# A two-stage image kernel on one core: the next image's norm, projection and lower levels moved into the last four units of the image before

## The chip, the cores and the metric

One core of a Trainium2 chip. The metric is the device time in microseconds (us) of one execution of the whole program on 16 images. PE is the matmul engine, DVE the vector engine, ACT the scalar engine, POOL the GpSimd engine, SP the engine that issues the DMAs here.

## The reference

x has shape (16, 256, 32, 32), float32. Two residual blocks follow each other:

```python
x = x + conv(gn(x))      # per image: softmax keys give a 7x7 filter for each channel, depthwise convolution
x = x + ssm_block(gn(x)) # gn: group norm, 32 groups
# ssm_block:
xz = in_w @ x; x, z = split(xz)          # 128 channels each
f1 = c1_w @ x                            # 1024 positions
f2 = conv2s2(f1); f3 = conv2s2(f2)       # 256 and 64 positions: the lower levels
# for each level and direction (6 scans), 16 states n:
delta = softplus(dt_w @ (xw @ f) + dtb)
h = h * exp(delta * A_n) + delta * B_n * f ; y += h * C_n
y = layernorm(y + D * f)
out = out_w @ (y1 * silu(z))             # y1 gathers the upsampled lower levels
```

## The kernel before, in words

The five engines run programs written out by hand and meet at counted semaphores. `stages` (L1424) calls a body for each image: 37 units (`NU`), then a bridge. A body works on three images at once: i is in its scans, j = i+1 is in its convolution, m = i+2 is in the preparation of its convolution weights. The bodies are (none, none, 0), (none, 0, 1), fourteen turns of a loop with all three, (14, 15, none) and (15, none, none). So image j's feature maps must be ready when the body's bridge ends, since its units come next.

A unit k is a part of image i's scans. Unit 0 is the third level (64 positions, all 16 states and both directions), units 1 to 4 the second level, units 5 to 36 the first level, one state and one direction each. In a unit:

- SP brings the rows B and C, broadcast to 128 partitions, into rings of 2 (bb) and 3 (cb); `get_b`, `get_c`.
- ACT computes exp(delta A) for unit k+1 in two halves (`decay`, L1173) into the PSUM tile slot_b. Each half waits until DVE's scan of unit k that reads the same bank is over.
- POOL multiplies B with u for unit k+1 (`inputs`, L1315 and L1318) and adds the products of unit k-1 to y (`gather`, L1338 and L1343).
- DVE runs two scans (`scan`, L552) and two products with C (`weigh`, L561).
- PE runs the convolution of image j as 98 taps of six matmuls (`taps`, L790; 14 rows of 7 taps); how many fall to a unit is set by `ROOM` and by `BRIDGE_TAPS`, whose last number is the taps that the bridge before has done. ACT makes the diagonal matrices of a row, 14 of them, in parts (`make_row`, `row_parts`, L1059); rows 0 to 2 and half of row 3 of image m are made in units 33 to 36.

`PREP` is 33, so the last four units are 33 to 36. The norms of image i's y (k = 0 to 3) lie in the units (the fourth, norm(3), in unit 33 on DVE), norms 4 and 5 in the bridge. Image j: in unit 33 DVE finishes the convolution (`conv_add`, L486) behind norm(3) and takes its statistics (`b_s0`, L431); in unit 34 PE sums them and ACT takes the spread (`gn_spread`, L958); in unit 35 ACT normalises (`b1`, L1105); in unit 36 PE projects f (L798). ACT copies f at the end of unit 36 (`copy_f`, L1112). Image m: `take_weights` (L1028) needs `conv_out` of j, `prep` (L1048) writes the high half of its padded image in unit 33, DVE the low half in unit 34 (`low_half`, L444; it waits for prep).

The bridge: PE computes the two lower levels (`lower`, L816), then chunk 0 (third level) and chunk 1 (second level) of delta, B and C (`chunk`, L831, L832), the centring and spread of norms 4 and 5 (L846, L852), z's projection (L807) and the output (L857). Each chunk is `chunk_exp` on ACT (from L1124, the last instruction is L1133), `chunk_first` on DVE (L500), `chunk_log` on ACT (L1139), `chunk_last` on DVE (L508, L510) and `chunk_low` on POOL (L1285). ACT's 16 decays of the third level (L1164) need chunk 0's delta; DVE's two scans of it (`scan_least`, L525) need these and POOL's product. `output` on DVE (L628) writes ob. ACT then makes the decays of unit 1, starts y, keeps x, makes more rows and copies the next x before its chunk 2. All engines' streams are in program order.

## Time and profile before

| | |
|---|---|
| median of 3 runs | 4224.79 us (4222.85 to 4224.82) |
| profiled execution, its time | 4222.54 us |
| its span in the profile | 4220.7 us |
| granted PE clock, mean | 0.873 of full |
| largest groups | L790 PE taps 2270.5 us; L1343 POOL y 1324.5; L1315 POOL bx 1220.1; L552 DVE scans 954.4 and 663.6 |

How to read it: a row of the timeline gives the start in us from the start of the span, the duration, the engine, the line of the kernel, what is written from what, and in brackets how long the engine was idle before and who released it. Rows of several instructions carry their count.

### The profile page before, as it was taken

The numbers are of one execution on the slowest core, as the hardware profiler recorded it, in microseconds if no ns is written. First come the engines' busy times: TensorE is split into PE (matmuls) and PEld (weight loads), VectorE is DVE, ScalarE is ACT, GpSimd is POOL, SyncE is SP. The second block draws the span as 40 slices with busy tenths as digits, with TensorE's granted clock in tenths as the row PEclk, the third lists the DMA queues.
The fourth block names the chain that finished last, engine by engine and source line by source line (L and its number), as shares of the span: only waits on it lengthen the run. The fifth ranks groups of instructions, "written<-read, shape, count | busy, mean of one in ns | idle before, by whom it ended". The sixth has DMA issues, their size and how long they took to land.

```text
span 4220.7 us, 53011 instructions
## 1 busy us (share of the span) xinstructions
PE 3109.9 (74%) x12620; PEld 1400.2 (33%) x12620; DVE 3209.0 (76%) x3975; ACT 2693.2 (64%) x6662; POOL 3290.3 (78%) x1908
## 2 busy tenths in 40 slices
PE   6978777887777788777777877788787778877511
PEld 3433333333333333333333433333333333333200
DVE  1058788787877878787887878788787887878877
ACT  4467766666766666666656766665677666666532
POOL 0059698796968969697896969889696987969797
PEclk8989888998888899889898988999898889988755
DMA  1025455453545545354553544445354554635544
GB/s 41 1 101 195 147 163 169 157 205 127 186 150 166 186 136 204 134 178 152 170 201 122 199 149 165 161 168 203 119 195 145 167 170 157 204 118 192 163 165 167
DMA packets 187275, 664.08 MB, mean 157 GB/s; under 512 B 22736, under 2 KB 24672, under 8 KB 186976
## 3 DMA queue, kind: packets, MB, share of 16 engines
q1 hardware_dynamic: 186976, 661.47, 46.4%
q14 instruction: 280, 2.29, 0.2%
q8 instruction: 19, 0.31, 0.0%
HBM read 639.76 MB, written 21.63 MB: 157 GB/s over the span
## 4 chain that ended last, share of the span: by engine, by line
POOL 28%; issue 19%; ACT 16%; PE 14%; DVE 13%; DMA 7%; POOLq 1%; DVEq 1%; SPq 0%; ACTq 0%
POOL bx L1315 13%; POOL y L1343 7%; DMA bb<-bc_rows 7%; ACT diag L1059 7%; PE pconv L790 6%; POOL h L1338 5%; DVE h L561 4%; DVE slot_c L552 2%; POOL bx L1318 2%; DVE rs L508 2%; ACT slot_b L1173 2%; PE pm L832 1%; PE pm L807 1%; PE pm L831 1%; DVE rs L500 1%
## 5 line engine op out<-in xcount | busy, mean ns | idle before, releaser
L790 PE MATMUL pconv<-pad,diag 128*128 128x512 f16 x9408 | 2270.5, 398 | 314.3 <-ACT diag L1059 210.0
L790 PEld LDWEIGHTS pconv<-pad,diag 128*128 128x128 f16 x9408 | 932.0, 100 | 1618.0 <-issue 346.0
L1343 POOL TENSOR_TENSOR y<-y,h 128x1024 f32<-128x1024 f32 (+2 forms) x672 | 1324.5, 1971 | 162.9 <-DVE h L561 139.6
L1173 ACT ACTIVATE slot_b<-delta,nega 128x512 f32<-128x512 f32 (+1 forms) x1280 | 805.4, 639 | 951.3 <-DVE slot_c L552 911.6
L1315 POOL TENSOR_TENSOR bx<-bb,u 128x1024 f32<-128x1024 f32 x512 | 1220.1, 2383 | 31.9 <-DMA bb<-bc_rows 31.9
L552 DVE TENSOR_TENSOR_SCAN slot_c<-slot_b,bx 128x512 f32<-128x512 f32 (+1 forms) x1024 | 954.4, 956 | 315.6 <-POOL bx L1315 214.6
L561 DVE TENSOR_TENSOR h<-slot_c,cb 128x512 f32<-128x512 f32 x1280 | 860.6, 674 | 35.9 <-POOL y L1343 35.9
L552 DVE TENSOR_TENSOR_SCAN slot_c<-slot_b,slot_c,bx 128x512 f32<-128x512 f32 x512 | 663.6, 1296 | 74.5 <-ACT slot_b L1173 18.2
L1059 ACT ACTIVATE diag<-id,chi 128x128 f16<-128x128 f16 x1568 | 498.1, 387 | 10.3 <-PE pconv L790 9.6
L1059 ACT ACTIVATE diag<-id,clo 128x128 f16<-128x128 f16 x1568 | 496.4, 386 | 0.0
L1338 POOL TENSOR_TENSOR h<-h 128x512 f32<-128x512 f32 (+3 forms) x384 | 349.9, 911 | 20.9 <-DVE h L531 3.4
L1285 POOL TENSOR_TENSOR delta<-delta,rs 128x512 f32<-128x512 f32 (+1 forms) x96 | 97.7, 1017 | 324.6 <-DVE rs L510 324.6
L1318 POOL TENSOR_TENSOR bx<-bb,u 128x1024 f32<-128x1024 f32 x64 | 158.8, 2482 | 125.5 <-DMA bb<-bc_rows 97.9
L500 DVE SCALAR_TENSOR_TENSOR rs<-qs,es 128x512 f32<-128x512 f32 (+1 forms) x96 | 64.9, 676 | 223.6 <-ACT qs L1133 223.6
L831 PE MATMUL pm<-f,wbc 128*32 128x512 f32 (+1 forms) x192 | 102.3, 620 | 147.0 <-ACT delta L1129 74.2
L1295 POOL TENSOR_TENSOR f<-f,lnw 128x98 f32<-128x98 f32 x16 | 6.2, 388 | 182.8 <-ACT f L1003 182.8
L1139 ACT ACTIVATE qs<-qs 128x512 f32<-128x512 f32 (+1 forms) x96 | 50.5, 526 | 153.7 <-DVE rs L500 153.7
L852 PE MATMUL pm<-es,ones 128*128 128x512 f32 (+1 forms) x128 | 62.7, 573 | 113.2 <-ACT es L1183 113.2
L846 PE MATMUL pm<-y,cen 128*128 128x512 f32 (+1 forms) x128 | 60.3, 554 | 89.2 <-POOL y L1343 40.6
L722 PE MATMUL pm<-ident,xh 128*128 128x128 f32 x256 | 47.0, 343 | 98.3 <-ACT xg L1094 72.1
L832 PE MATMUL pm<-f,wdelta 128*128 128x512 f32 (+1 forms) x192 | 116.9, 698 | 0.0
L695 PE MATMUL pconv<-sg,grp 128*128 128x8 f32 x32 | 9.5, 371 | 145.5 <-DVE sg L431 145.5
(171 smaller groups left out, 3095.9 us busy)
## 6 DMA issues: line engine op xcount, KB each, us to landing
bb<-bc_rows SPq DMA_DIRECT2D x592, 512.0 KB, 4.4
cb<-bc_rows SPq DMA_DIRECT2D x592, 512.0 KB, 4.4
xr<-in_x SPq DMA_DIRECT2D x16, 1024.0 KB, 5.0
out<-ob SPq DMA_DIRECT2D x16, 1024.0 KB
bc_rows<-rows SPq DMA_DIRECT2D x64, 64.0 KB, 1.6
w<-in_w SPq DMA_DIRECT2D x2, 256.0 KB
wc<-in_wc SPq DMA_DIRECT2D x2, 256.0 KB
bc_rows<-rows SPq DMA_DIRECT2D x16, 32.0 KB, 4.0
```

The lines of the kernel that those rows point to most:

```text
L500: nc.vector.scalar_tensor_tensor(er[:, k, 0:n], qs[:, k, 0:n], 1.0, es[:, k, 0:n], ALU.subtract, ALU.subtract).then_inc(ch_err.sem, 1)
L552: ins = nc.vector.tensor_tensor_scan(hv, av, bv, start, ALU.mult, ALU.add)
L561: nc.vector.tensor_tensor(half(h[:, q % HR], b), bank(slot_c, b), half(cb[:, k % CR], b), ALU.mult).then_inc(q_pr.sem, 1)
L790: ins = nc.tensor.matmul(bank(pconv, k), w, pad[:, t, part, rows:rows + 16, dx:dx + W], start=first and m == 0, stop=last and m == 2)
L831: nc.tensor.matmul(bank(pm, 0)[0:2 * NS, 0:n], wbc[:, st, :], f[:, fc:fc + n], start=True, stop=True).then_inc(ch_bc.sem, 1)
L832: nc.tensor.matmul(bank(pm, 1)[:, 0:n], wdelta[:, st, :], f[:, fc:fc + n], start=True, stop=True).then_inc(ch_dt.sem, 1)
L1059: ins = nc.scalar.activation(diag[:, r % RING, m, dx, :], id16[:, :], ACT.Copy, scale=(chi, clo)[m][:, t, dy * KK + dx:dy * KK + dx + 1])
L1173: ins = nc.scalar.activation(slot_b[:, o:o + w], delta[:, so + c:so + c + w], ACT.Exp, scale=nega[:, st, n0 + n:n0 + n + 1])
L1315: ins = pool.tensor_tensor(bx[:, k % 2, :], bb[:, k % BR, :], us, ALU.mult)
L1318: ins = pool.tensor_tensor(o, bb[:, k % BR, :].rearrange("p (m l) -> p m l", m=m), us[:, None, :].to_broadcast([P, m, ln]), ALU.mult)
L1338: pool.tensor_tensor(src[:, 0:m], src[:, 0:m], src[:, m:2 * m], ALU.add).then_inc(n_y.sem, 1)
L1343: pool.tensor_tensor(yv, yv, src[:, 0] if len(src.shape) == 3 else src, ALU.add).then_inc(q_y.sem, 1)
```

## The change

The statistics of image j move ahead of unit 33's scans on DVE, and PE's sums, the spread and the whole normalisation on ACT into unit 33; f's projection into unit 34; the lower levels and the three copies of f into units 35 and 36; chunk 0 into unit 36. On DVE chunk_first(j, 0) stands ahead of unit 36's scans. ACT's prep moves from unit 33 to unit 34. In the bridge ACT makes the 16 decays of the third level and DVE runs its first scan ahead of norm 4, the second ahead of the output. SP issues the first B rows before it waits for the last products. Of image m's taps 1 stays in unit 35, unit 36 does 3 (before 2), the bridge 7 (before 6), so 11 instead of 9 are done when unit 0 begins; that shifts a few of the other taps, and rows 9 and 10 of the diagonal matrices come one and two units earlier (11 and 15 instead of 12 and 17).

```diff
@@ -337,7 +337,7 @@
 
             if k == 4:
                 return bank(delta, 0), bank(delta, 1), bank(delta, 2)
-            return bank(delta, 3), half(h[:, 0], 0), half(h[:, 0], 1)
+            return bank(delta, 3), half(h[:, 2], 0), half(h[:, 2], 1)
 
         def half(ap, b):
             return ap[:, b * HALF:(b + 1) * HALF]
@@ -399,9 +399,10 @@
                     if i is not None:
                         sp.wait_ge(u_bx.sem, u_bx.at(j, 0))
                         sp.sem_inc(sp_held, 1)
+                    get_b(j, 0)
+                    if i is not None:
                         sp.wait_ge(q_pr.sem, q_pr.at(j, 0))
                         sp.sem_inc(sp_held, 1)
-                    get_b(j, 0)
                     get_c(j, 0)
                     put_rows(j, 1)
                     get_b(j, 1)
@@ -631,28 +632,30 @@
 
             def bridge(i, j, m):
                 if j is not None:
-                    chunk_first(j, 0)
-                if j is not None:
-                    chunk_last(j, 0)
+                    chunk_first(j, 1)
+                    scan_least(j, 0)
                 if i is not None:
                     norm(i, 4)
                 if j is not None:
-                    chunk_first(j, 1)
+                    chunk_last(j, 1)
                 if i is not None:
                     norm(i, 5)
                 if j is not None:
-                    chunk_last(j, 1)
+                    scan_least(j, 1)
                 if i is not None:
                     output(i, 0)
                     output(i, 1)
                 if j is not None:
                     silu_clip(j)
-                    scan_least(j, 0)
-                    scan_least(j, 1)
 
             pre = {3: a_s0, 17: a_max_, 19: a_dg_, 20: a_ktc_, 21: a_fic_, 22: a_f2c_, 27: a_scale_}
 
             def unit(i, j, m, k):
+                if j is not None and k == PREP:
+                    conv_add(j, 1)
+                    b_s0(j)
+                if j is not None and k == NU - 1:
+                    chunk_first(j, 0)
                 if i is not None:
                     products(i, k)
                     if k in CHUNK_FIRST:
@@ -665,13 +668,11 @@
                     pre[k](m)
                 if j is not None and k == HALF_AT:
                     conv_add(j, 0)
-                if k == PREP:
-                    if j is not None:
-                        conv_add(j, 1)
-                        b_s0(j)
                 if k == PREP + 1:
                     if m is not None:
                         low_half(m)
+                if j is not None and k == NU - 1:
+                    chunk_last(j, 0)
 
             stages(unit, bridge, dve)
 
@@ -861,30 +862,23 @@
                 def some(lo, hi):
                     if m is not None:
                         taps(m, BRIDGE_TAPS[lo], BRIDGE_TAPS[hi])
+                if j is not None:
+                    chunk(j, 1)
                 some(2, 3)
-                if j is not None:
-                    lower(j, 0)
+                if i is not None:
+                    norm_centre(i, 4)
+                    norm_centre(i, 5)
                 some(3, 4)
-                if j is not None:
-                    lower(j, 1)
+                if i is not None:
+                    norm_spread(i, 4)
+                    norm_spread(i, 5)
                 some(4, 5)
                 if j is not None:
-                    chunk(j, 0)
-                if i is not None:
-                    norm_centre(i, 4)
-                    norm_centre(i, 5)
-                if j is not None:
-                    chunk(j, 1)
-                if i is not None:
-                    norm_spread(i, 4)
-                    norm_spread(i, 5)
-                some(5, 6)
-                if j is not None:
                     project_z(j)
                 if i is not None:
                     output(i, 0)
                     output(i, 1)
-                some(6, 7)
+                some(5, 6)
 
             pre = {5: lambda m: sums1(m, sa, pm, a_sums, a_stats), 6: lambda m: sums2(m, sa, pm, a_sums, a_spread),
                    15: a_key_, 16: lambda m: (a_turn(m, 0), a_turn(m, 1)), 17: lambda m: (a_turn(m, 2), a_turn(m, 3)),
@@ -895,24 +889,31 @@
                 mid = min(hi, lo + (FIRST_TAPS if 2 <= k < 5 else 1))
                 if j is not None:
                     taps(j, lo, mid)
-                if m is not None and k == PREP + 2:
-                    taps(m, 0, BRIDGE_TAPS[1])
                 if i is not None:
                     if k in CHUNK_PE:
                         chunk(i, CHUNK_PE[k])
                 if j is not None:
                     taps(j, mid, hi)
-                    if k == PREP + 1:
+                    if k == PREP:
                         sums1(j, sg, pconv, b_sums, b_stats)
                         sums2(j, sg, pconv, b_sums, b_spread)
+                if j is not None and k == PREP + 1:
+                    if i is not None:
+                        pe.wait_ge(n_o.sem, n_o.at(i, STEPS[4]))
+                    if m is not None:
+                        pe.wait_ge(a_w16.sem, a_w16.at(m, 1))
+                    project_f(j, 0)
+                    project_f(j, 1)
+                if k == PREP + 2:
+                    if j is not None:
+                        lower(j, 0)
+                    if m is not None:
+                        taps(m, 0, BRIDGE_TAPS[1])
+                    if j is not None:
+                        lower(j, 1)
                 if k == PREP + 3:
                     if j is not None:
-                        if i is not None:
-                            pe.wait_ge(n_o.sem, n_o.at(i, STEPS[4]))
-                        if m is not None:
-                            pe.wait_ge(a_w16.sem, a_w16.at(m, 1))
-                        project_f(j, 0)
-                        project_f(j, 1)
+                        chunk(j, 0)
                     if m is not None:
                         taps(m, BRIDGE_TAPS[1], BRIDGE_TAPS[2])
                 if m is not None and k in pre:
@@ -1098,8 +1099,10 @@
                 act.wait_ge(a_max.sem, a_max.at(j, 1))
                 nc.scalar.activation(ex[:, :], ex[:, :], ACT.Exp, bias=sk[:, 0:1], accum_out=sk[:, 1:2]).then_inc(a_exp.sem, 1)
 
-            def b1(i):
+            def b_root(i):
                 gn_root(act_b, i, sg, pconv, b_sums, b_total, b_var, b_rstd, b_shift)
+
+            def b_normal(i):
                 act.wait_ge(b_shift.sem, b_shift.at(i, 1))
                 for t in range(CT):
                     nc.scalar.activation(xg[:, t, :], xn[:, t, :], ACT.Identity, scale=sg[:, 54 + t:55 + t],
@@ -1197,23 +1200,15 @@
 
             def bridge(i, j, m):
                 if j is not None:
-                    copy_f(j, 1)
-                    copy_f(j, 2)
-                    chunk_exp(j, 0)
+                    chunk_exp(j, 1)
+                    decay(j, 0, 0)
+                    chunk_log(j, 1)
                 if i is not None:
                     norm_square(i, 4)
-                if j is not None:
-                    chunk_log(j, 0)
-                if i is not None:
                     norm_square(i, 5)
-                if j is not None:
-                    chunk_exp(j, 1)
-                if i is not None:
                     norm_root(i, 4)
                     norm_root(i, 5)
                 if j is not None:
-                    chunk_log(j, 1)
-                    decay(j, 0, 0)
                     if i is not None:
                         act.wait_ge(b_g.sem, b_g.at(j, 0))
                     copy_z(j)
@@ -1235,26 +1230,38 @@
                    23: a_spread_, 24: a_norm_, 25: a_relu_, 26: a_w_, 27: a_split_}
 
             def unit(i, j, m, k):
-                if j is not None and k == PREP + 1:
-                    act_b.start(act, j)
-                    gn_spread(act_b, j, sg, pconv, b_sums, b_spread)
-                if j is not None and k == PREP + 2:
-                    b1(j)
                 if i is not None:
                     if k in CHUNK_LAST:
                         chunk_log(i, CHUNK_LAST[k])
-                    if 1 <= k < NU - 1:
-                        decay(i, k + 1, 0)
                 if m is not None and k == PREP:
                     take_weights(m)
                     act.wait_ge(c_w.sem, c_w.at(m, 1))
-                row_parts(j, m, k, 0)
+                if j is not None and k == PREP:
+                    row_parts(j, m, k, 0)
+                    act_b.start(act, j)
+                    gn_spread(act_b, j, sg, pconv, b_sums, b_spread)
+                if i is not None:
+                    if 1 <= k < NU - 1:
+                        decay(i, k + 1, 0)
+                if j is not None and k == PREP:
+                    b_root(j)
+                else:
+                    row_parts(j, m, k, 0)
+                if j is not None and k == PREP + 2:
+                    copy_f(j, 0)
                 if i is not None:
                     if 1 <= k < NU - 1:
                         decay(i, k + 1, 1)
+                if j is not None and k == PREP:
+                    b_normal(j)
+                if j is not None and k == PREP + 2:
+                    copy_f(j, 1)
                 if j is not None and k == PREP + 3:
-                    copy_f(j, 0)
+                    copy_f(j, 2)
+                    chunk_exp(j, 0)
                 row_parts(j, m, k, 1)
+                if j is not None and k == PREP + 3:
+                    chunk_log(j, 0)
                 if i is not None:
                     if k in CHUNK_PE:
                         chunk_exp(i, CHUNK_PE[k])
@@ -1269,7 +1276,7 @@
                 if m is not None:
                     if k in pre:
                         pre[k](m)
-                    if k == PREP:
+                    if k == PREP + 1:
                         prep(m)
 
             stages(unit, bridge, act)
@@ -1374,7 +1381,7 @@
 
 TAPS = NR * KK
 PREP = NU - 4
-BRIDGE_TAPS = (0, 1, 3, 3, 3, 3, 6, 9)
+BRIDGE_TAPS = (0, 1, 4, 5, 6, 8, 11)
 FIRST_TAPS = 2
 
 
```

## Rows read from the trace of the kernel before

**Rows 1.** The page: busy time of each engine, share of the span
```profile
PE 3109.9 (74%) x12620; PEld 1400.2 (33%) x12620; DVE 3209.0 (76%) x3975; ACT 2693.2 (64%) x6662; POOL 3290.3 (78%) x1908
```

**Rows 2.** Timeline of POOL: start, us, engine, line, operation, [idle before, releaser]
```profile
1981.49 2.35 POOL L1343 TENSOR_TENSOR y<-y,h 128x1024 f32<-128x1024 f32 x1 [0.67 <-DVE h L561]
...
2025.58 1.27 POOL L1285 TENSOR_TENSOR delta<-delta,rs 128x512 f32<-128x512 f32 x1 [3.38 <-DVE rs L510]
...
2230.21 2.35 POOL L1343 TENSOR_TENSOR y<-y,h 128x1024 f32<-128x1024 f32 x1 [0.67 <-DVE h L561]
```

**Rows 3.** Timeline, PE and DVE, last four units of one image
```profile
1950.47 2.83 PE L790 MATMUL pconv<-pad,diag 128*128 128x512 f16 x12
...
1952.68 1.23 DVE L552 TENSOR_TENSOR_SCAN slot_c<-slot_b,bx 128x512 f32<-128x512 f32 x1
...
1958.88 1.28 DVE L486 SCALAR_TENSOR_TENSOR xn<-pconv,csc,xn 128x1024 f32<-128x1024 f32 x1
...
1962.59 1.21 DVE L552 TENSOR_TENSOR_SCAN slot_c<-slot_b,bx 128x512 f32<-128x512 f32 x1
...
1966.30 4.96 DVE L444 TENSOR_TENSOR pad<-xh,pad 128x1024 f16<-128x1024 f32 x2
...
1971.18 1.22 DVE L552 TENSOR_TENSOR_SCAN slot_c<-slot_b,bx 128x512 f32<-128x512 f32 x1
...
1972.65 2.72 PE L790 MATMUL pconv<-pad,diag 128*128 128x512 f16 x6 [4.96 <-ACT sg L973]
...
1976.49 1.23 DVE L552 TENSOR_TENSOR_SCAN slot_c<-slot_b,bx 128x512 f32<-128x512 f32 x1 [1.51 <-ACT slot_b L1173]
```

**Rows 4.** Timeline, ACT, the same units and the start of the bridge
```profile
1960.25 0.29 ACT L1028 ACTIVATE chi<-whi 128x98 f32<-128x98 f16 x1 [5.61 <-DVE xn L486]
...
1963.80 2.01 ACT L1048 ACTIVATE pad<-xh 128x1024 f16<-128x1024 f32 x2
...
1970.67 1.26 ACT L1059 ACTIVATE diag<-id,chi 128x128 f16<-128x128 f16 x4
...
1973.34 2.37 ACT L1105 ACTIVATE xg<-xn,sg 128x1024 f32<-128x1024 f32 x2
...
1975.61 0.67 ACT L1173 ACTIVATE slot_b<-delta,nega 128x512 f32<-128x512 f32 x1
...
1986.01 0.45 ACT L1112 ACTIVATE f<-pm,vec 128x256 f32<-128x256 f32 x1
...
1987.66 0.31 ACT L1112 ACTIVATE f<-pm,vec 128x64 f32<-128x64 f32 x1 [1.20 <-PE pm L816]
...
1989.43 0.26 ACT L1133 ACTIVATE qs<-es 128x64 f32<-128x64 f32 x1
```

**Rows 5.** Timeline, ACT, PE and DVE in the bridge
```profile
1989.64 0.60 ACT L1183 ACTIVATE delta<-slot_b 128x512 f32<-128x512 f32 x1
...
1991.48 1.02 PE L852 MATMUL slot_b<-delta,ones 128*128 128x512 f32 x2
...
1993.18 0.67 ACT L1194 ACTIVATE delta<-slot_b,eps 128x512 f32<-128x512 f32 x1
...
1994.55 0.70 DVE L603 TENSOR_TENSOR slot_b<-slot_b,delta 128x512 f32<-128x512 f32 x1 [3.64 <-ACT delta L1196]
```

**Rows 6.** Timeline, PE, ACT and DVE, later in the same bridge
```profile
1997.25 3.60 PE L807 MATMUL pm<-xg,wz 128*128 128x512 f32 x8
1997.45 3.91 ACT L1164 ACTIVATE a<-delta,nega 128x64 f32<-128x64 f32 x16
...
2003.46 1.61 DVE L628 SCALAR_TENSOR_TENSOR ob<-slot_c,vec,xc 128x512 f32<-128x512 f32 x2
...
2005.10 1.67 ACT L1173 ACTIVATE slot_b<-delta,nega 128x256 f32<-128x256 f32 x4 [2.74 <-DVE ob L628]
...
2006.17 4.53 DVE L525 TENSOR_TENSOR_SCAN h<-a,b 128x1040 f32<-128x1040 f32 x2
```

**Rows 7.** Windows: us, busy (count) of PE, PEld, DVE, ACT, POOL, PEclk, DMA
```profile
1968.00:1973.00 5.00, 0.35 (x1) 0.14 (x2) 4.98 (x3) 4.90 (x20) 2.18 (x1) 0.50 0.01 2
```

More of the change, by code:

```diff
@@ L863, in some @@
                         taps(m, BRIDGE_TAPS[lo], BRIDGE_TAPS[hi])
+                if j is not None:
+                    chunk(j, 1)
                 some(2, 3)
-                if j is not None:
-                    lower(j, 0)
-                some(3, 4)
-                if j is not None:
-                    lower(j, 1)
-                some(4, 5)
-                if j is not None:
-                    chunk(j, 0)
                 if i is not None:
@@ L875, in bridge @@
                     norm_centre(i, 5)
-                if j is not None:
-                    chunk(j, 1)
+                some(3, 4)
                 if i is not None:
@@ L880, in bridge @@
                     norm_spread(i, 5)
-                some(5, 6)
+                some(4, 5)
                 if j is not None:
```

## Prediction

> **What bounds the kernel now.** I read the page first: POOL is busy for 78% of the span, DVE 76%, PE 74% and ACT 64% [rows 1], so no engine fills the span and the loss has a place. POOL's timeline over one loop turn shows it. The last product of an image starts at 1981.49 and that of the next at 2230.21: 248.7 us for an image. From 2025.58, where chunk 2's delta arrives, POOL runs nearly back to back; before that it idles again and again [rows 2]. So an image costs what POOL must do in its units, plus the stretch from the last four units to 2025.58, in which POOL waits. I follow that stretch on the engines it waits for.
>
> In units 33 to 36 DVE starts its scans at 1952.68, 1962.59, 1971.18 and 1976.49; between them lie norm 3, the end of the convolution with its statistics (1958.88 to 1962.59, 3.7 us) and the two subtractions of image m (1966.30 to 1971.18, 4.9 us). A unit of DVE without extras takes 3.8 to 4.3 us. PE's last taps of image j end at 1950.47 + 2.83 = 1953.3 [rows 3]. ACT works without a pause from 1960.25, when the convolution is out, to 1986.0, and chunk 0's last activation ends at 1989.7 [rows 4]. The bridge then runs norm 4 at 1994.55, the output's second half from 2003.46 to 2005.07, and ACT's next decays at 2005.10 [rows 5, 6]. From there ACT alone sets the time to 2025.58. So the number to forecast is when the output is over, "the handover": 2005.1 now. All that follows it is the same work and moves with it.
>
> **The change, worked out on the same clock (1950 to 2020).** All durations are from the rows named.
>
> 1. *Unit 33.* DVE now takes the convolution's end first. It would be free at 1952.68, but PE's last tap ends at 1953.3, so it waits 0.7 us, takes 3.7 us and scans at 1957.1 instead of 1952.7. The whole of the unit, 9.9 us of the same work [rows 3], ends at 1963.3. POOL's product behind it waits some 2 us; that is covered, because POOL idles further on anyway.
>
> 2. *ACT, units 33 and 34.* The convolution is out 5.5 us sooner, so ACT starts at 1954.7 instead of 1960.25. Up to the first decay of unit 36 it worked 1975.61 - 1960.25 = 15.4 us without a gap [rows 4]. The new order has the same instructions ahead of prep's end, and one decay more (0.6 us): 16.0. But the sums now go DVE, PE, ACT, PE, ACT with little between them. I put these waits at 2.2 us, an estimate; the bounds are nothing and 4 us, twice the gaps I can lay out. Prep, which now stands last in unit 34, so ends at 1954.7 + 16.0 + 2.2 = 1972.9, its first half 1 us sooner.
>
> 3. *The first new wait.* DVE has done unit 34's scans at 1963.3 + 3.9 = 1967.2, and its next instruction is the subtraction that needs prep's first half, at 1971.9. It stands still for 4.7 us; before, prep was over (1963.80 + 2.02) by the time DVE came (1966.30) [rows 3, 4]. The subtraction ends at 1976.8, unit 35's first scan at 1978.0. Behind that scan waits ACT's first decay of unit 36: ACT, done at 1972.9, stands still for 5.1 us. Queued behind that decay are the rest of the rows and the copies of f.
>
> 4. *ACT, units 35 and 36.* The old stretch from 1975.61 to 1986.0 (10.4 us: two decays, 28 diagonals, one copy) less the last 8 diagonals (2.3; four take 1.17 [rows 4]) is 8.1 us. The wait for PE's lower level adds 1.4 (the third copy waited 1.2 [rows 4]; the second level is larger), the second copy 0.5: the third copy starts at 1978.1 + 10.0 = 1988.1. From there to chunk 0's last activation the rows give 1989.69 - 1987.66 = 2.0 us. It ends at 1990.1, against 1989.7 before. So chunk 0, the aim of the move, comes at the same time.
>
> 5. *The second new wait.* chunk_first(j, 0) stands ahead of unit 36's scans on DVE. DVE has done unit 35 at 1976.8 + 3.9 = 1980.7 and waits to 1990.1, 9.4 us. Behind it are unit 36's scans, their products, and POOL's last two sums. Scans and products take 4.9 - 0.5 = 4.4 us [rows 2, 3], chunk_first 0.3: over at 1994.8. POOL's last sum runs from 1995.0 to 1997.4. Before, it ended at 1983.8 [rows 2]. This costs the tail what the head was to gain.
>
> 6. *The bridge.* POOL's chunk 0 delta 0.3 us: 1997.7. ACT's 16 decays 3.9 us [rows 6]: 2001.7. chunk 1's logarithm 0.4 (an estimate: 256 columns, where 512 take 0.67), the square 0.6, PE's spread 1.0, logarithm and root 1.3 (two of 0.67) [rows 5]: norm 4 starts at 2005.2. DVE: norms 4 and 5 together 4.3 (six instructions of 0.7), chunk_last 0.9 (two of half that width), the second long scan 2.3 (two take 4.53), the output 3.3 (two halves of 1.61) [rows 5, 6], in all 10.8: the handover is at 2016.0. PE beside it: 12 taps 2.8, z 3.6, output 1.9 after the spread at 2004.7, in time by 0.3 us at the full clock. SP's first B rows go out at 1989 or so and land before 1997.7; nothing gained, nothing lost. The long scans that left the end of the bridge shorten only DVE's wait before chunk 2, since ACT sets that time.
>
> So the handover comes 2016.0 - 2005.1 = **10.9 us later** in each of the 14 loop turns.
>
> 7. *PE's clock.* In the middle of the stretch PE idles and its clock is granted at half, 1.2 GHz: the window 1968 to 1973 has 0.50 [rows 7], and six tap matmuls there take 2.72 us, where twelve took 2.83 at full rate [rows 3]. After the change PE idles around 1953 to 1964, again from 1968 to 1981, and in the bridge between chunk 1 and the norms. At half rate throughout, taps, z and output take 8.3 us more, and of that 8 would show: upper bound 8 us a turn. Lower bound nothing. I take 1.6, since a stretch of PE's work follows the idle time in which the clock can rise, as it did at 1972.65 to 1979.
> The Trainium skill ("TensorE: Matmul & The Clock Gate", Part 1) says that the half rate is the default state, that sustained activity releases it and idleness brings it back, and that for a typical kernel the ramp is under 1% of the span. The trace agrees on the levels; 1% would be 42 us as an estimate, where my term makes 14 x 1.6 = 22.
>
> 8. *The rest.* The turn without image m (14, 15) has no prep, so the first new wait is absent; the second is there. I take 6.5 us, between 0 and 10.9. The first image's turns have no scans to hold up: 0, between -3 and 3. Rows 9 and 10 of the diagonals come earlier and ahead of chunks 4 and 5 on ACT; ACT waits for DVE in those units, so 0, between -1 and 2 us an image.
>
> **Sum.** 14 x (10.9 + 1.6) + 6.5 = 181.5 us on the profiled execution's own 4222.5 us (span 4220.7): 4404. The median of the runs is 2.3 us above it: **4406 us**, 4.3% slower.
>
> **Rivals.**
> *A. The first wait does not show* (prep comes before DVE, because ACT has idle time I have not seen). For it: ACT is 5.5 us ahead at the start. Against: 16.0 us of its work stand ahead of prep's end. Then chunk 0 comes 5.1 us sooner, the second wait shrinks to 4.3, the handover is 5.8 later: 14 x 5.8 + 6 = 87, 4312 us.
> *B. Faster.* If chunk 0's last activation is over when DVE comes to unit 36 as early as before (1976.5), neither wait exists, the last sum ends at 1983.8 as before, and the bridge, 18.6 us from there to the handover, ends at 2002.4: 2.7 sooner, 14 x 2.7 = 38, **4187 us**. It decides at step 5: chunk 0 must come 13.6 us sooner than I find. Against it speaks that ACT's own work from 1954.7 to there is 26 us.
> *C. Little change*: the later units' slack takes up what the handover loses, 4225. Against: POOL is busy for 3290.3 / 16 = 206 us an image [rows 1], nearly what 2025.58 to the turn's end holds; there is little slack to give [rows 2].
> *D. PE's clock stays low through the bridge*, by the rule above: 14 x 18.9 + 6.5 = 271, 4496 us. For it: three idle stretches. Against: the taps between.
>
> **How the numbers follow.** Forecast 0.58, A and cases near it 0.14, B 0.08, C 0.04, D and near it 0.16. The range from 4310 to 4490 takes in A, the bounds of steps 2 and 8 and most of D, and leaves out B, C and the rest of D. Slower by over 0.2% (8.4 us, about what a measurement of this kernel can tell from no change): 0.88; within: 0.04; faster: 0.08.
>
> **What would show it.** Right: a loop turn of about 261 us; DVE idle some 5 us before L444 (released by ACT's L1048) and some 9 us before the first L500 (released by ACT's L1133) with unit 36's scans right behind it; POOL's last sum 13 us later against the last taps; ACT idle about 5 us before a decay behind L444; z or the output's matmuls at half rate now and then. Wrong: unit 36's scans start without a wait, or the 16 decays come before the last sum, or the end of ACT's prep lies before DVE's unit 34.

## The result, and the profile after

The changed kernel takes 4404.92 us (median of 4 runs, 4399.67 to 4405.99), the kernel before 4223.82 (median of 4, 4221.43 to 4224.82): ratio 1.0427, 95% interval 1.0409 to 1.0445. The forecast was 4406, slower. The profiled spans are 4402.8 and 4220.7: 182.1 us more. First the page's busy line, which answers to [rows 1]:

```profile
PE 3192.7 (73%) x12620; PEld 1438.2 (33%) x12620; DVE 3223.9 (73%) x3975; ACT 2695.9 (61%) x6662; POOL 3277.5 (74%) x1908
```

DVE, ACT and POOL are busy for the same time within 15 us. PE has 83 us more for the same instructions, and its mean granted clock is 0.860 instead of 0.873. None of this adds up to 182 us on one engine: most of the time is in waits.

**Where it goes, by image.** The output DMA marks the handover of each image. I read its start for all 16 images in both traces:

```
                                before    after    more
first handover                  506.2     530.6    24.4   (+12.6 in the first fill, +11.8 in the first turn)
13 turns, mean of one           249.46    261.26   13 x 11.8 = 153.4
turn 14 -> 15 (no image m)      235.4     245.0     9.6
last image, to its output       231.8     226.4    -5.4
```

The first fill is taken to end where ACT makes the decays of unit 1 of the first image: at 256.3 before and at 268.9 after. So each of the 14 loop turns is 11.8 us longer, where the forecast had 10.9 + 1.6 = 12.5.

**Where it goes within a turn.** The handover is at 2097.51 in the turn shown. The timeline of PE, ACT, DVE and POOL in the changed kernel, with the columns of [rows 2], first the four units:

```profile
2035.29 1.28 DVE L487 SCALAR_TENSOR_TENSOR xn<-pconv,csc,xn 128x1024 f32<-128x1024 f32 x1 [1.08 <-PE pconv L791]
...
2052.36 2.01 ACT L1049 ACTIVATE pad<-xh 128x1024 f16<-128x1024 f32 x2
2053.45 2.37 DVE L445 TENSOR_TENSOR pad<-xh,pad 128x1024 f16<-128x1024 f32 x2 [4.30 <-ACT pad L1049]
...
2056.99 0.69 ACT L1176 ACTIVATE slot_b<-delta,nega 128x512 f32<-128x512 f32 x1 [2.61 <-DVE slot_c L553]
...
2060.52 3.78 PE L817 MATMUL pm<-f,wc 128*128 128x256 f32 x8 [9.05 <-ACT f L1115]
...
2064.33 0.47 ACT L1115 ACTIVATE f<-pm,vec 128x256 f32<-128x256 f32 x1 [3.29 <-PE pm L817]
...
2068.79 0.29 ACT L1115 ACTIVATE f<-pm,vec 128x64 f32<-128x64 f32 x1
...
2070.53 0.26 ACT L1136 ACTIVATE qs<-es 128x64 f32<-128x64 f32 x1
2070.70 1.26 ACT L1060 ACTIVATE diag<-id,clo 128x128 f16<-128x128 f16 x4
2070.82 0.23 DVE L501 SCALAR_TENSOR_TENSOR rs<-qs,es 128x64 f32<-128x64 f32 x1 [11.28 <-ACT qs L1136]
2071.10 1.23 DVE L553 TENSOR_TENSOR_SCAN slot_c<-slot_b,bx 128x512 f32<-128x512 f32 x1
```

Both new waits are there. DVE stands still 4.30 us before the subtraction (L445), released by ACT's pad, and 11.28 us before chunk 0's first step (L501), released by ACT's qs, with unit 36's scans right behind it. Between them ACT waits 2.61 us for DVE, then 3.29 for PE's lower level. These eight matmuls took 3.78 us where they took 2.01 before; their windows, with a row of before under that of after:

```profile
2060.50:2064.00 3.50, 3.48 (x8) 2.63 (x9) 0.00 (x0) 0.54 (x1) 0.00 (x0) 0.50 0.00 0
```
```profile
1983.80:1985.80 2.00, 1.98 (x8) 1.42 (x8) 0.00 (x0) 2.00 (x8) 0.04 (x1) 1.00 0.00 0
```

The granted clock (the column after POOL's) is 0.50 here and was 1.00. Before, PE's longest idle time of this stretch, 9.42 us, stood ahead of the small sums of image j's norm; now the longest, 9.05 us, stands just ahead of matmuls for which ACT waits. Then the bridge:

```profile
2073.07 2.36 POOL L1350 TENSOR_TENSOR y<-y,h 128x1024 f32<-128x1024 f32 x1 [13.02 <-DVE h L562]
...
2075.67 2.35 POOL L1350 TENSOR_TENSOR y<-y,h 128x1024 f32<-128x1024 f32 x1 [0.24 <-DVE h L562]
2075.67 2.42 DVE L511 TENSOR_TENSOR rs<-rs,es 128x64 f32<-128x64 f32 x1
...
2078.64 3.93 ACT L1167 ACTIVATE a<-delta,nega 128x64 f32<-128x64 f32 x16 [1.98 <-POOL delta L1292]
...
2082.70 2.32 DVE L526 TENSOR_TENSOR_SCAN h<-a,b 128x1040 f32<-128x1040 f32 x1 [4.27 <-ACT a L1167]
...
2085.80 3.88 PE L791 MATMUL pconv<-pad,diag 128*128 128x512 f16 x12
2085.95 0.70 DVE L604 TENSOR_TENSOR slot_b<-slot_b,delta 128x512 f32<-128x512 f32 x1 [0.93 <-ACT delta L1199]
...
2089.51 3.59 PE L808 MATMUL pm<-xg,wz 128*128 128x512 f32 x8
...
2092.94 1.88 PE L858 MATMUL slot_b<-o,wo 128*128 128x512 f32 x4
```

POOL's last sum ends at 2078.0. From there to the handover it is 19.5 us; it was 21.4 (1983.8 to 2005.24, [rows 2]), so the bridge gained nearly 2 us, and the last sum came later by more than that. From the start of the convolution's end (L487) to the handover it is 62.2 us here and 46.4 before; from the handover to the next L487 199.5 on average, before 202.8. The head, which was to gain the 5.5 us of a unit, gained 3.3.

The turn shown is one of the longer ones: the 12 taps before z (3.88 us) run partly at half rate in it. In the turns where they run at the full rate they take 2.76 us, and norm 4 to the handover takes 10.2 us instead of 11.6. Over 13 turns the stretch from L487 to the handover is 15.3 us longer on average (61.8 for 46.5): 0.4 up to the first copy of f, 4.4 between the first and the third copy of f, nothing from there to chunk 0's first step (L501), 10.2 from that to norm 4, and 0.3 from norm 4 to the handover.

### The profile page after: what moved, and what is told of

The parts are those of the page before. It is cut to its first block, busy times and chain, and to the rows that moved or that the text cites. A ratio compares the mean times of both kernels' runs of the same rounds, so it can differ in the third digit from the quotient of the medians.

```text
span 4402.8 us, 53011 instructions
## 1 busy us (share of the span) xinstructions
PE 3192.7 (73%) x12620; PEld 1438.2 (33%) x12620; DVE 3223.9 (73%) x3975; ACT 2695.9 (61%) x6662; POOL 3277.5 (74%) x1908
## 4 chain that ended last, share of the span: by engine, by line
ACT 22%; POOL 19%; DVE 18%; issue 17%; PE 17%; DMA 4%; DVEq 1%; POOLq 0%; SPq 0%; ACTq 0%
PE pconv L791 9%; ACT diag L1060 9%; POOL bx L1322 8%; POOL y L1350 5%; DVE h L562 5%; DMA bb<-bc_rows 4%; DVE slot_c L553 4%; POOL h L1345 3%; ACT slot_b L1176 2%; POOL bx L1325 2%; DVE rs L511 2%; DVE rs L509 2%; ACT a L1167 1%; DVE rs L501 1%; PE pm L817 1%
## 5 line engine op out<-in xcount | busy, mean ns | idle before, releaser
L791 PE MATMUL pconv<-pad,diag 128*128 128x512 f16 x9408 | 2295.4, 401 | 327.1 <-ACT diag L1060 248.7
L791 PEld LDWEIGHTS pconv<-pad,diag 128*128 128x128 f16 x9408 | 941.5, 101 | 1648.9 <-issue 324.7
L1322 POOL TENSOR_TENSOR bx<-bb,u 128x1024 f32<-128x1024 f32 x512 | 1205.7, 2355 | 24.6 <-DMA bb<-bc_rows 24.6
L1060 ACT ACTIVATE diag<-id,chi 128x128 f16<-128x128 f16 x1568 | 498.3, 387 | 12.7 <-PE pconv L791 12.2
L501 DVE SCALAR_TENSOR_TENSOR rs<-qs,es 128x512 f32<-128x512 f32 (+1 forms) x96 | 82.9, 863 | 260.4 <-ACT qs L1136 258.5
L1325 POOL TENSOR_TENSOR bx<-bb,u 128x1024 f32<-128x1024 f32 x64 | 157.7, 2465 | 153.2 <-DMA bb<-bc_rows 125.8
L817 PE MATMUL pm<-f,wc 128*128 128x256 f32 (+1 forms) x256 | 74.5, 450 | 136.7 <-ACT f L1115 136.7
L799 PE MATMUL pm<-xg,wf 128*128 128x512 f32 x128 | 98.9, 944 | 55.2 <-DVE o L589 28.3
L723 PE MATMUL pm<-ident,xh 128*128 128x128 f32 x256 | 59.4, 409 | 95.6 <-ACT ex L1091 60.7
L511 DVE TENSOR_TENSOR rs<-rs,es 128x512 f32<-128x512 f32 (+1 forms) x96 | 125.8, 1310 | 3.3
```

The source lines that it names most:

```text
L501: nc.vector.scalar_tensor_tensor(er[:, k, 0:n], qs[:, k, 0:n], 1.0, es[:, k, 0:n], ALU.subtract, ALU.subtract).then_inc(ch_err.sem, 1)
L511: nc.vector.tensor_tensor(er[:, k, 0:n], er[:, k, 0:n], es[:, k, 0:n], ALU.min).then_inc(ch_min.sem, 1)
L791: ins = nc.tensor.matmul(bank(pconv, k), w, pad[:, t, part, rows:rows + 16, dx:dx + W], start=first and m == 0, stop=last and m == 2)
L817: ins = nc.tensor.matmul(pm[:, o:o + n], w[:, m, :], src[:, :, m // 2, :, m % 2], start=(m == 0), stop=(m == 3))
L1060: ins = nc.scalar.activation(diag[:, r % RING, m, dx, :], id16[:, :], ACT.Copy, scale=(chi, clo)[m][:, t, dy * KK + dx:dy * KK + dx + 1])
L1322: ins = pool.tensor_tensor(bx[:, k % 2, :], bb[:, k % BR, :], us, ALU.mult)
```

## The experiments

Twelve kernels. Undone means that this edit alone is put back as it was before. One turn is the mean of thirteen. "conv to out" is from L487 to the handover, "out to conv" the rest of the turn (of four turns in the middle of the trace). The kernel before took 4223.8 us beside the changed kernel, 4221.9 beside e1, e2, e4 and e6, 4225.7 beside e3, e5, e7 and e8, and 4221.9 beside e9 to e12, so differences between rows are good to some 4 us:

```
                                     us        to after   a turn   conv to out   out to conv
before                              4222-4226             249.5    46.4          202.8
after                               4404.9               261.3    61.0-62.2     199.5
e1  chunk 0 behind the scans        4374.0     -31       260.0    58.8-61.9     199.3-200.7
e2  prep in unit 33                 4380.4     -25       259.7    59.4-60.4     199.7
e3  e1 and e2                       4370.9     -34       259.6    60.0          199.4
e4  norms 4, 5 first                4366.6     -38       259.3    58.9          200.6
e5  e1, e2, e4                      4313.5     -91       255.7    54.4-56.2     199.7
e6  PE kept busy, short             4406.2      +1       260.8    60.5-62.1     199.4
e8  PE kept busy, long              4386.2     -19       259.6    59.1-60.6     199.9
e7  9 rows of taps, not 11          4372.3     -33       258.8    61.0-62.0     196.2-198.4
e9  e5 and e7                       4236.5    -168       250.5    52.0-55.0     196.8
e10 e9, chunk 1 ahead of the taps   4254.5    -150       251.5    54.1-55.7     196.7
                                               to before
e11 before, 11 rows of taps         4257.0     +35       251.8    46.4          204.3-206.2
e12 before, scans ahead of norms    4278.8     +57       252.8    50.7          201.9
```

**e1: the second wait.** On DVE, chunk 0's first step is put behind unit 36's products:

```diff
-                if j is not None and k == NU - 1:
-                    chunk_first(j, 0)
                 if i is not None:
                     products(i, k)
+                if j is not None and k == NU - 1:
+                    chunk_first(j, 0)
```

> The changed kernel, with DVE's chunk_first(j, 0) moved behind unit 36's scans and products (the second wait taken away). Theory: the 11.3 us that DVE stands still before L501 go, POOL's last sum ends some 10 us sooner, but the 16 decays then wait for the end of chunk 1's activations on ACT (2076.7 in the turn read) instead of chunk 0's delta (2078.6), so the handover gains only 2.0 us a turn: 28 us less than the changed kernel, about 4377. Rival (the wait is on the path with its whole length): 11 us a turn, 158 us less, about 4247.

Measured 4374.04 (4373.55 to 4381.6), ratio to before 1.0361 (1.0344 to 1.0378): 31 us, near the theory's 28. The scans no longer wait:

```profile
2053.65 1.23 DVE L553 TENSOR_TENSOR_SCAN slot_c<-slot_b,bx 128x512 f32<-128x512 f32 x1
2054.59 3.78 PE L818 MATMUL pm<-f,wc 128*128 128x256 f32 x8 [8.99 <-ACT f L1116]
...
2064.90 0.23 DVE L501 SCALAR_TENSOR_TENSOR rs<-qs,es 128x64 f32<-128x64 f32 x1 [6.85 <-ACT qs L1137]
...
2070.65 3.91 ACT L1168 ACTIVATE a<-delta,nega 128x64 f32<-128x64 f32 x16
```

DVE does unit 36 in the time in which it waited, and then waits for the same qs, 6.85 us instead of 11.28. The profiled run is the slowest of the four (4381.6); its turn is 1.25 us shorter and the turn 14 to 15 4.7; by the medians it is 31 / 14 = 2.2 us a turn. The wait is worth no more, because the 16 decays start 5.75 us behind L501, where it was 7.82: as the theory had it, they no longer wait for POOL's chunk 0 delta, but stand behind chunk 1's activations on ACT. Nor is the wait for chunk 0 itself new. In the kernel before DVE had waited at the same instruction, with unit 36's scans already done:

```profile
1989.71 0.23 DVE L500 SCALAR_TENSOR_TENSOR rs<-qs,es 128x64 f32<-128x64 f32 x1 [8.38 <-ACT qs L1133]
```

**e2: the first wait.** ACT's prep goes back from unit 34 to unit 33 (`k == PREP + 1` becomes `k == PREP`).

> The changed kernel, with ACT's prep back at the end of unit 33 (the first wait taken away). Theory: DVE's 4.3 us before the subtraction go or shrink below 1 us, ACT's 2.6 us before unit 36's first decay go, chunk 0 comes 2.6 us sooner and the handover with it: 36 us less, about 4369. Rival (the first wait is hidden behind the second): no change, 4405.

Measured 4380.38 (4377.63 to 4382.65), ratio 1.0375 (1.0358 to 1.0392): 25 us of the 36 expected.

```profile
2039.32 4.98 DVE L445 TENSOR_TENSOR pad<-xh,pad 128x1024 f16<-128x1024 f32 x2
2039.88 3.33 POOL L1322 TENSOR_TENSOR bx<-bb,u 128x1024 f32<-128x1024 f32 x1
...
2059.32 0.23 DVE L501 SCALAR_TENSOR_TENSOR rs<-qs,es 128x64 f32<-128x64 f32 x1 [11.29 <-ACT qs L1136]
```

The wait before the subtraction is gone, but the subtraction itself takes 4.98 us again, as in [rows 3], where in the changed kernel it took 2.37. Earlier by 4.3 us, it falls on POOL's product bx, which takes 3.33 us instead of 2.35. So the price of 4.9 us that the prediction read from before belongs to a collision that the new wait had removed.

**e3: both.** The edits of e1 and e2 together.

> The changed kernel, with both new waits of DVE taken away at once: prep back in unit 33 and chunk_first(j, 0) behind unit 36's scans. Theory: with prep in unit 33 the 16 decays already started only 0.3 us behind the end of chunk 1's activations, so taking the second wait away too gains next to nothing more: 4376 (4372 to 4381). Rival (the two waits add): 25 us and 31 us less than the changed kernel, 4349.

Measured 4370.89 (4369.41 to 4372.47), ratio 1.0345 (1.0328 to 1.0362). 31 and 25 make 34, near the theory's 29 and far from the rival's 56. Up to chunk 0 the gain of e2 stays whole; what is lost is e1's gain behind it. The 18 taps ahead of chunk 1, in e3 and then in e1:

```profile
2053.79 5.82 PE L792 MATMUL pconv<-pad,diag 128*128 128x512 f16 x18
```
```profile
2063.72 4.21 PE L792 MATMUL pconv<-pad,diag 128*128 128x512 f16 x18
```

The granted clock in these stretches is 0.70 and 1.00. So in e3 chunk 1 comes later, and the decays, which stand behind it on ACT, start 7.3 us behind L501 (mean of 13 turns) where it is 6.1 in e1; from L501 to the handover it is 26.2 and 24.7 us. These 1.5 us a turn, 21 us in all, are an estimate of what the lower clock takes from e3; no run removes it there.

**e4: the bridge's order.** Norms 4 and 5 ahead of the decays and long scans again, on ACT and on DVE:

```diff
 (ACT)               chunk_exp(j, 1)
-                    decay(j, 0, 0)
-                    chunk_log(j, 1)
                 if i is not None:
                     norm_square(i, 4) ... norm_root(i, 5)
                 if j is not None:
+                    chunk_log(j, 1)
+                    decay(j, 0, 0)
 (DVE)           both scan_least behind silu_clip
```

> The changed kernel, with norms 4 and 5 ahead of the third level's decays on ACT and ahead of both its scans on DVE, as in the kernel before; all else as changed. Theory: the logarithm of norm 4 starts at 2080.4 instead of 2084.6 and the handover comes 4.1 us sooner in each turn, the scans fall where ACT sets the time: 57 us less, about 4348. Rival (PE's taps, z and output set the handover): at most 1 us a turn, 4391 or more.

Measured 4366.56 (4362.03 to 4371.77), ratio 1.034 (1.0323 to 1.0357): 38 us of the 57 expected. From L501 to the handover it is 22.8 us instead of 26.7 in the turn shown, the 4 us expected; but that turn is one of the longer ones of the changed kernel, "out to conv" is 1.0 longer, and the mean turn of the profiled run (the slowest of the four) gains 1.9 us. The long scans stand behind the output again, and the theory had put them at nothing there; e12, which takes them away from there, sees "out to conv" 0.9 shorter.

**e12: the bridge's order, put into the kernel before.** The same move from the other side: in the kernel before, decays and chunk 1's logarithm ahead of the roots, chunk_first(j, 1) and the first long scan ahead of norm 4, the second behind norm 5. The buffer `h[:, 2]` of a norm comes with it, as in the change.

> The kernel before with only its bridge reordered: third-level decays ahead of the norms' roots on ACT, the first long scan ahead of norm 4 and the second behind norm 5 on DVE, ahead of the output. Theory: ACT's decays (3.9) and chunk 1's logarithm (0.4) delay the roots by 4.3, norm 4 starts at 1999.5 instead of 1994.55, and the two scans of 2.3 stand ahead of the output: handover 5 us later, 14 x 5.0 = 70, 4294. Rival: what the scans no longer take behind the output is given back there, 4225.

Measured 4278.8 (4273.53 to 4284.66), ratio 1.0139 (1.0122 to 1.0156): 57 us of the 70 expected.

```profile
2011.96 3.91 ACT L1164 ACTIVATE a<-delta,nega 128x64 f32<-128x64 f32 x16
...
2015.99 2.32 DVE L525 TENSOR_TENSOR_SCAN h<-a,b 128x1040 f32<-128x1040 f32 x1 [3.49 <-ACT a L1164]
2018.24 0.67 DVE L603 TENSOR_TENSOR slot_b<-slot_b,delta 128x512 f32<-128x512 f32 x1
```

Norm 4 (L603) waits behind the scan, which waits for the decays; "conv to out" is 4.35 us longer, of which the turn gives back 1. So this part by itself is slower by 1.4%. It is 3.3 us a turn, of the 11.8.

**e6 and e8: PE's clock.** Both put matmuls of no use ahead of the lower level, so that PE isn't idle there; e6 twice more project_f in unit 34, e8 nine projections of 512 columns (recorded as 18 matmuls) into pconv in unit 35.

> The changed kernel, with f's projection computed three times over in unit 34 (the same matmuls into the same banks, two of the three thrown away), so that PE is busy up to the lower level. Theory: the clock is at its full rate when the lower level comes, its first eight matmuls take 2.0 us instead of 3.8, the second copy of f comes 1.8 us sooner, and so does the handover: 25 us less, about 4380. Rival (the clock costs nothing on the path): 4405, or more by what the extra matmuls hold up.

> The changed kernel, with nine matmuls of 512 columns more on PE in unit 35, right ahead of the lower level, into the bank pair of the convolution, which is free then and written anew by the next tap. In the run before with the projection computed three times PE still stood still for 2.2 us ahead of the lower level and the granted clock there was 0.53. Theory (the half clock costs 1.8 us of the path at the lower level): the clock is full there, the eight matmuls take 2.0 us, chunk 0 comes 1.8 us sooner: 4380. Rival: the same as the changed kernel, 4405, because the rows of diagonals or the decays of the bridge set the end.

e6: 4406.21 (4405.53 to 4410.09), ratio 1.0441 (1.0423 to 1.0458). e8: 4386.23 (4385.47 to 4390.05), ratio 1.0383 (1.0365 to 1.04). The lower level of e6, then that of e8 with what ran ahead of it:

```profile
2056.47 3.64 PE L817 MATMUL pm<-f,wc 128*128 128x256 f32 x8 [2.21 <-ACT f L1120]
```
```profile
2043.78 7.89 PE L911 MATMUL pconv<-xg,wf 128*128 128x512 f32 x18
...
2052.96 2.02 PE L817 MATMUL pm<-f,wc 128*128 128x256 f32 x8 [1.29 <-ACT f L1118]
```

e6 did not test what it was made for: with 2.2 us idle ahead of it, the lower level still took 3.64 us, so its time says nothing of the clock's price. In e8 it takes 2.02 us, 1.8 less, and the turn is 1.7 us shorter (the turn 14 to 15 is 5.9 longer; what the added matmuls hold up there was not read). So the half rate of the lower level lies on the path almost whole. The Trainium skill ("TensorE: Matmul & The Clock Gate", Part 1) says that the half rate is the default and idleness brings it back; both levels show here.

**e7: the rows of taps.** `BRIDGE_TAPS = (0, 1, 4, 5, 6, 8, 11)` becomes `(0, 1, 3, 4, 4, 6, 9)`: two rows (12 matmuls) fewer before unit 0 of the next image. The spread of the other rows over the units follows from it.

> The changed kernel, with as many taps done before unit 0 as in the kernel before (BRIDGE_TAPS 0, 1, 3, 4, 4, 6, 9), so that rows 9 and 10 of the diagonals are made in units 12 and 17 again. Theory: the stretch from one handover to the last tap loses the 1.5 us it had gained in length, 15 to 25 us less: about 4385. Rival (that stretch is longer for another reason, as the DVE's and POOL's state at the handover): 4400 to 4410.

Measured 4372.25 (4366.96 to 4376.85), ratio 1.0349 (1.0332 to 1.0366). The theory's 4385 was short and the rivals' 4400 to 4410 further off: 33 us, 2.5 a turn, and it is "out to conv" that is shorter. Where in it, e11 shows.

**e11: the rows of taps, put into the kernel before.** `(0, 1, 3, 3, 3, 3, 6, 9)` becomes `(0, 1, 3, 3, 3, 3, 6, 11)`.

> The kernel before with only the two further rows of taps behind the output (11 rows ahead of unit 0 instead of 9). Theory: two rows are 12 matmuls of 0.24 us each, 2.8 us on PE between the output and chunk 2's projections, and with ACT's earlier diagonals they lie on the path: 14 x 2.4 = 33, 4258. Rival, as the prediction had it: no cost, 4224.

Measured 4256.97 (4254.8 to 4262.49), ratio 1.0086 (1.0069 to 1.0103), the number expected. But the reason is another. "conv to out" stays at 46.36 us, and behind the output 36 tap matmuls stand (8.10 us) where 24 took 5.43; yet chunk 2's first step on DVE comes 17.39 us behind the handover in both kernels, so they cost nothing there. DVE's scans fall behind all at once, by 3.3 us in the turn shown, 64 to 69 us after the handover. The kernel before, then e11:

```profile
2066.60 2.74 PE L790 MATMUL pconv<-pad,diag 128*128 128x512 f16 x6 [12.40 <-ACT diag L1059]
...
2069.14 0.43 PE L695 MATMUL pm<-sa,grp 128*128 128x8 f32 x2
```
```profile
2081.51 6.35 PE L790 MATMUL pconv<-pad,diag 128*128 128x512 f16 x18 [17.77 <-ACT diag L1059]
...
2087.70 0.28 PE L695 MATMUL pm<-sa,grp 128*128 128x8 f32 x2
...
2088.02 0.17 ACT L958 ACTIVATE sa<-pm 128x4 f32<-128x4 f32 x1 [3.36 <-PE pm L695]
...
2089.74 1.23 DVE L552 TENSOR_TENSOR_SCAN slot_c<-slot_b,bx 128x512 f32<-128x512 f32 x1 [3.73 <-ACT slot_b L1173]
```

PE stands still 17.77 us for diagonals, and then has 18 tap matmuls instead of 6 ahead of the two small sums of image m's norm (L695), at a granted clock of 0.62. ACT waits 3.36 us for these sums with its next decays behind them, and DVE's scan waits for a decay. The changed kernel shows the same place, 18 taps of 6.20 us and waits of 3.21 and 3.57 us, and e7 has 6 taps of 2.74 us there and neither wait.

**e5, e9, e10: what is left.** e5 undoes e1, e2 and e4 together; e9 undoes the rows of taps too.

> The changed kernel, with both waits taken away and norms 4 and 5 ahead of the decays and scans. Theory: norm 4 then starts right behind chunk 1's activations, 5 us a turn sooner than with both waits away alone, the turn is about 254.7 us and the time about 4306, still above the kernel before. Rival (the order in the bridge and the two waits are the whole loss): 4225.

> The changed kernel with four edits undone: chunk 0's first step behind unit 36's scans, prep back in unit 33, norms 4 and 5 ahead of the decays and the two long scans as before, and nine rows of taps in the last four units and the bridge instead of eleven. With the first three alone the time was 4313.5, and the rows of taps alone gave 33 us. Theory: taps ahead of chunk 1 and the norms stand on the path in every order, so the two gains add: 4280 (4270 to 4290). Rival: with the other three undone the taps are hidden behind ACT's work: 4313, as without the edit.

e5: 4313.48 (4312.77 to 4314.3), ratio 1.0209 (1.0192 to 1.0226). e9: 4236.52 (4235.89 to 4239.37), ratio 1.0037 (1.0023 to 1.0051). e5 came near its theory (4306), which refutes its rival of 4225. e9 missed both of its values, by 43 us and more. The rows of taps alone were worth 33 us, on top of e5 77; e4 alone 38, on top of e3 57. The 77 are 2.7 us a turn in "out to conv", as in e7, and 2.6 in the bridge, where norm 4 comes 12.4 us behind L501 in e5 and 9.5 in e9: with the norms first, the taps ahead of chunk 1 are no longer hidden. With all four undone, 182 us become 14. The head is then 6.0 us shorter than before, 196.8 instead of 202.8, as the move was to bring, but "conv to out" is still 52 to 55 us against 46.4. Its timeline shows what eats the gain:

```profile
1982.38 3.78 PE L817 MATMUL pm<-f,wc 128*128 128x256 f32 x8 [6.99 <-ACT f L1115]
...
1986.20 0.47 ACT L1115 ACTIVATE f<-pm,vec 128x256 f32<-128x256 f32 x1 [3.30 <-PE pm L817]
...
1990.66 0.29 ACT L1115 ACTIVATE f<-pm,vec 128x64 f32<-128x64 f32 x1
...
1992.69 0.23 DVE L501 SCALAR_TENSOR_TENSOR rs<-qs,es 128x64 f32<-128x64 f32 x1 [6.84 <-ACT qs L1136]
```

The lower level runs at half rate and ACT waits 3.30 us for it. Between the second and the third copy of f ACT forms diagonals for 4.0 us, 1.2 of it after PE's second level had ended (1989.4). Before, the two copies stood 1.65 us apart [rows 4]. No run takes these diagonals away, so their share is argued, not shown.

The spread of "conv to out" in e9 has another source. Here are the 12 taps ahead of chunk 1 in a turn whose "conv to out" is 54.9 us, and in one where it is 52.0:

```profile
1740.56 5.33 PE L791 MATMUL pconv<-pad,diag 128*128 128x512 f16 x12
```
```profile
2242.11 2.83 PE L791 MATMUL pconv<-pad,diag 128*128 128x512 f16 x12
```

The granted clock is 0.50 in the first and 1.00 in the second. The turns with the full rate there are 249.0 us long, 0.5 shorter than before; the mean of e9 is 250.5. So 1.5 us a turn, 20 us in all by this estimate, go with the clock in these taps, more than the 14 by which e9 is slower. No run holds the clock up there. SP's new order was not undone in any run either.

e10 is e9 with chunk 1's projections moved ahead of unit 36's taps.

> The kernel e9 with chunk 1's two projections ahead of the last unit's taps instead of behind them, so that ACT's wait for them (2.8 us where 18 taps stood before them) goes. Theory: PE's own sequence (taps, then the norms' centring) sets when norm 4 starts, so nothing comes of it: within 8 us of e9, 4280. Rival: ACT's wait for chunk 1 is what delays the squares and roots, and 14 x 2.8 = 39 us are won: 4241.

Measured 4254.54 (4249.72 to 4255.12), ratio 1.0074 (1.0057 to 1.0091): neither value; beside e9 it costs 18 us.

```profile
2004.97 0.59 PE L832 MATMUL pm<-f,wbc 128*32 128x256 f32 x2 [0.70 <-ACT delta L1131]
...
2007.65 0.36 ACT L1126 ACTIVATE rows<-pm 32x256 f32<-32x256 f32 x1
...
2011.68 1.02 PE L847 MATMUL slot_b<-y,cen 128*128 128x512 f32 x2
```

ACT no longer waits for chunk 1 (no bracket at rows; 1.41 us in e9), as the rival wanted. But chunk 1's matmuls now wait 0.70 us for ACT to free pm, and all 18 taps stand between them and the norms' centring, in 5.73 us at a granted clock of 0.71; at the full rate 18 take 4.21. From L501 to the centring it is 6.8 us here and 5.3 in e9 (means of 13 turns), and the turn is 1.05 longer. Another 6.2 us of the 18 come with the first handover; what does it there is open.

## Why the prediction was right, point by point

The sign, the mechanism and the size held: two waits on DVE in series with ACT's chain, a bridge that puts the decays on the path, 11.8 us a turn for 12.5. That the sum came within 2 us of the measured one is luck: its terms were off in both directions, and two of them, the rows of taps and the subtraction, by 2.4 and 2.5 us a turn.

- *Step 1* held in form. DVE waited 1.08 us before the convolution's end, not 0.7. But the head gained 3.3 us of the 5.5, since unit 33 itself is reached later: step 8 had set the rows of taps at 0, and e7 and e11 show 2.4 to 2.5 us a turn for them. That is the largest term missed, with +35 us in e11 against a bound of 2 us an image. Step 8 looked at ACT's diagonals; what it left out is PE's taps ahead of image m's sums.
- *Steps 2 and 3.* The first wait was 4.30 us (forecast 4.7), ACT's behind it 2.61 (5.1). The step that failed is the subtraction's price: 2.37 us, not 4.9, as POOL's bx had ended (2051.98) before it began. Rival A, that the first wait doesn't show, is refuted by its row, and e2 bounds its worth: 25 us, where A had 94.
- *Step 4.* From ACT's start behind the convolution (1954.7 in the forecast) to chunk 0's last activation it was to be 35.4 us, and was 34.1 (2036.67 to 2070.79). The parts differ: ACT's wait for the lower level was 3.29 us, not 1.4, for the clock; the subtraction gave 2.5 back.
- *Step 5.* The wait was 11.28 us, not 9.4. POOL's last sum ended 12.2 us later against the last taps, forecast 13. "This costs the tail what the head was to gain" was too strong: by e1 it costs 2.2 us a turn.
- *Step 6.* DVE's chain of 10.8 us from norm 4 to the handover took 11.4 (2085.95 to 2097.36, where ACT's decays follow). ACT's order put norm 4 where the step had it: 7.9 us behind the last sum, forecast 7.8 (the terms as written give 2005.0, not 2005.2). e4 and e12 show the order to be the dearest single part, 38 and 57 us. That the long scans would give nothing back behind the output was wrong: by e12 it is 0.9 us a turn.
- *Step 7.* The clock was put at 1.6 us a turn, in the bridge. e8 shows 1.7 at another place, the lower level. In the bridge the 12 taps took 3.88 us instead of 2.8 in the turn shown (granted clock 0.62 from 2085 to 2089), and z started at 2089.51 behind them; DVE waited 0.68 us for the output's matmuls. In the middle of the trace this is so in every other turn, so the clock takes some 0.8 us a turn there by estimate; with the 1.7 that is 2.5 where the step had 1.6.
- *Step 8.* Turn 14 to 15: 9.6 for 6.5. First fill: 12.6 for 0, outside the bound of 3. Last image: -5.4, which wasn't in the sum. There ACT has no work for a next image and DVE set the start, before; its two long scans (4.82 us) are now over at the handover. These three sum to +16.8 where the forecast had 6.5; the 14 turns make 165.2 where it had 175.

Rival B (faster) needed chunk 0 some 13 us sooner; it came 1.3 sooner than forecast. e9 comes nearest to it: with the orders and taps of before, the move is 0.4% slower. Rival C (4225) is refuted by the time itself. Rival D had 18.9 us a turn: PE's clock was low at the lower level and in part of the taps, but z (3.59 us) and the output (1.88) ran at the full rate.

## What to carry to other kernels

The move brought the next image's head forward by some 6 us a turn once the taps were put back (e9), and lost them again in the bridge. A wait in a profile is worth what is left when the next one takes over: 11.3 us of DVE's idle time were worth 2.2, and two edits of 31 and 25 us gave 34 together, while two others gave far more together than alone. So test the parts both ways, taken out of the new kernel and put alone into the old one; the part that looks like filling (two more rows of taps where PE "has time") cost 35 us by itself, and not where the taps were added but 65 us later, where they pushed other taps ahead of two small sums. A number that comes out as expected doesn't show the reason: find the place in the trace where the two kernels part. And when work is moved ahead on one engine, look at what the others were doing at the new moment: the same subtraction costs 2.4 or 5 us, the same eight matmuls 2.0 or 3.8.

## What the hardware showed that was not expected

**DVE and POOL hold each other up.** The two subtractions took 2.37 us while POOL stood still, and 4.96 to 4.98 us beside a POOL product of 128x1024, which itself took 3.33 instead of 2.35 (e2's rows above). The single record of e2's pair shows 1.69 and 3.37 us. A DVE operation of 128x64 that takes 0.22 us took 2.42 when it started at the same moment, 2075.67, as a POOL sum of 2.35 us (rows of after). DVE thus seems to wait for POOL's whole instruction. The Trainium skill ("SBUF — State Buffer", "SBUF: two separate sides") says this: the pair of ports shared by DVE and GpSimd is an exclusive lock, held for a whole instruction, also against a DVE operation with two SBUF inputs. The trace agrees for the 2.42 us and for the second subtraction, which ends 1.1 us after POOL's product does. The first subtraction started 0.56 us ahead of that product and still took 1.69 us instead of 1.18, which the rule alone doesn't explain; no run here settles it. The forecast had read 4.9 us of such a pair as the price of work that takes 2.37.

**The clock falls where the new wait is.** PE's idle time of 9.05 us ahead of the lower level was followed by the half rate (granted clock 0.50). In e6 PE ran at the full rate from 2048 to 2054.3 (1.00), stood still for 2.2 us, and the eight matmuls behind it took 3.64 us at 0.53. In e8 1.29 us of idle time behind 7.9 us of matmuls were followed by the full rate (1.00).
